# A skip sum moved from GpSimd to VectorE in the last layer of a graph network

## The reference

```python
x = _layernorm(x + attention(x, adj))          # stage 1
skip = x
for l in range(3):                             # stage 2, L = 3 layers
    si, sj = x @ attn_w[l, :d], x @ attn_w[l, d:]
    scores = leaky(si[:, :, None] + sj[:, None, :] + attn_b[l])
    attn = softmax(where(mask, scores, -inf))
    h = layernorm(x + attn @ x, g1[l], beta1[l])
    ff = gelu(h @ W1[l] + b1[l]) @ W2[l] + b2[l]
    x = layernorm(h + ff, g2[l], beta2[l])
out = _layernorm(skip + x)                     # the skip sum, its statistics, its normalization
```

## Time and profile before

| | before |
|---|---|
| median of 3 runs | 1709.91 us (1709.25 to 1709.99) |
| the profiled execution's own time | 1712.13 us |
| its span, first to last instruction | 1710.3 us |
| busy share of the span | PE 94%, DVE 77%, ACT 72%, POOL 78% |
| granted TensorE clock, mean | 0.98 |

### The profile page before, as it was taken

The page is one execution under the profiler, slowest core; times in us unless marked ns, Lnnn a source line. Parts: engine busy times, 40 slices in busy tenths (PEclk is TensorE's granted clock), DMA queues, the critical chain, the costliest instruction groups (busy, mean ns, idle before and its releaser), DMA issues.

```text
span 1710.3 us, 40177 instructions
## 1 busy us (share of the span) xinstructions
PE 1609.1 (94%) x11904; PEld 1425.8 (83%) x11904; DVE 1320.2 (77%) x5300; ACT 1230.9 (72%) x2855; POOL 1337.6 (78%) x2385
## 2 busy tenths in 40 slices
PE   4999999984999999999999999999999999999994
PEld 3888888872898998998898998988889888888894
DVE  1898898896777777777977777777888887888862
ACT  1888888883677677677777777776776777777763
POOL 5688888875478777787787787787778999999996
PEclk8999999996999999999999999999999999999997
DMA  6122332232022122122122221221220212222211
GB/s 200 64 93 93 98 98 90 87 106 80 26 99 91 44 74 74 37 74 73 38 75 72 88 74 38 72 74 37 74 73 26 86 65 95 74 74 79 69 50 49
DMA packets 145979, 127.50 MB, mean 75 GB/s; under 512 B 16512, under 2 KB 136832, under 8 KB 145920
## 3 DMA queue, kind: packets, MB, share of 16 engines
q1 hardware_dynamic: 138880, 124.30, 22.5%
q10 hardware_dynamic: 7040, 2.51, 0.6%
HBM read 89.04 MB, written 37.75 MB: 74 GB/s over the span
## 4 chain that ended last, share of the span: by engine, by line
PE 56%; POOL 13%; DVE 5%; issue 2%; ACT 1%; POOLq 0%; DVEq 0%; ACTq 0%
PE ps L45 24%; PE ps L894 24%; PE ps L866 4%; PE ps L880 2%; DVE gnn_junk L1026 2%; POOL xo L807 2%; POOL gnn_n L160 2%; POOL gnn_norm L801 2%; POOL gnn_fin L821 2%; POOL gnn_norm L160 2%; POOL inv L155 1%; PE ps L858 1%; POOL gnn_hb L790 1%; PE ps L873 1%; POOL gnn_hb L786 1%
## 5 line engine op out<-in xcount | busy, mean ns | idle before, releaser
L894 PE MATMUL ps<-gnn_w_hi,gnn_g_hi 128*128 128x256 f32 x1536 | 433.9, 282 | 0.0
L894 PE MATMUL ps<-gnn_w_lo,gnn_g_hi 128*128 128x256 f32 x1536 | 428.9, 279 | 0.0
L894 PE MATMUL ps<-gnn_w_hi,gnn_g_lo 128*128 128x256 f32 x1536 | 428.7, 279 | 0.0
L993 ACT ACTIVATE gnn_g_hi<-ps,b_cols 128x512 fp32r<-128x512 f32 x384 | 264.3, 688 | 200.1 <-PE ps L45 200.1
L1097 DVE TENSOR_TENSOR gnn_g_lo<-ps,gnn_g_hi 128x512 fp32r<-128x512 f32 x384 | 262.4, 683 | 101.6 <-ACT ps L994 101.0
L45 PE MATMUL ps<-gnn_hT_hi,gnn_w_hi 128*128 128x512 f32 x768 | 338.4, 441 | 0.0
L45 PE MATMUL ps<-gnn_hT_hi,gnn_w_lo 128*128 128x512 f32 x768 | 303.5, 395 | 0.0
L45 PE MATMUL ps<-gnn_hT_lo,gnn_w_hi 128*128 128x512 f32 x768 | 303.4, 395 | 0.0
L894 PEld LDWEIGHTS ps<-gnn_w_lo,gnn_g_hi 128*128 128x128 f32 x1536 | 288.9, 188 | 2.2
L894 PEld LDWEIGHTS ps<-gnn_w_hi,gnn_g_hi 128*128 128x128 f32 x1536 | 288.8, 188 | 2.2
L894 PEld LDWEIGHTS ps<-gnn_w_hi,gnn_g_lo 128*128 128x128 f32 x1536 | 288.7, 188 | 0.0
(11 more groups left out here) (127 smaller groups left out, 3979.4 us busy)
## 6 DMA issues: line engine op xcount, KB each, us to landing
hist<-xo SPq DMA_DIRECT2D x48, 512.0 KB, 3.9
x<-hist SPq DMA_DIRECT2D x48, 512.0 KB, 3.8
aw<-in_L_gnn_attn_w SPq DMA_DIRECT2D x48, 256.0 KB, 4.1
gmask<-mask_hist SPq DMA_DIRECT2D x48, 256.0 KB, 4.1
att_xT_raw<-in_xT SPq DMA_DIRECT2D x16, 512.0 KB, 3.3
att_xl<-in_x SPq DMA_DIRECT2D x16, 512.0 KB, 3.6
gnn_fin<-hist SPq DMA_DIRECT2D x16, 512.0 KB, 3.8
out<-gnn_fin SPq DMA_DIRECT2D x16, 512.0 KB, 3.0
```

What stands on the lines that cost most here:

```text
L894: mm = e.matmul(FF2[j % 2], g[a][:, m, j * N:(j + 1) * N], W2[b][:, m, :], start=(n == 0), stop=(n == len(terms) - 1))
L993: e.activation(g[0][:, m, :], FF1[FFB[m]], ACT.Gelu, bias=bias)
```

## The change

`final_sum` is taken out of POOL's step. `final_statistics(t-1)` on DVE, in step t, now waits for the load of `fin` and for `xo` of step t-1 (`x_out`), writes a one-column fence, makes the four sums itself, and then takes the statistics, each behind a wait for its sum. The wait for `fin_sum` is thus one within DVE.

```diff
-                def final_sum(t, par, half):
-                    e.wait_ge(fin_ld[par], 16 * (half - FIRST // 2 + 1))
-                    for j in range(GROUP):
-                        ins = e.tensor_tensor(fin[par][:, j, :], fin[par][:, j, :], xo[par][:, j, :], ALU.add)
-                    ins.then_inc(fin_sum, 1)
...
                     ln_ffn(2 * q + par, par, q, final >= 1)
-                    if final >= 1:
-                        final_sum(2 * q + par, par, q)
...
                 def final_statistics(q, par):
-                    t1, p1, _ = ahead(q, par, -1)
+                    t1, p1, h1 = ahead(q, par, -1)
                     n = t1 - FIRST
-                    e.wait_ge(fin_sum, n + 1)
-                    for j in range(GROUP):
+                    e.wait_ge(fin_ld[p1], 16 * (h1 - FIRST // 2 + 1))
+                    hold_dve(e, x_out, t1 + 1)
+                    for j in range(GROUP):
+                        e.tensor_tensor(fin[p1][:, j, :], fin[p1][:, j, :], xo[p1][:, j, :], ALU.add).then_inc(fin_sum, 1)
+                    for j in range(GROUP):
+                        e.wait_ge(fin_sum, GROUP * n + j + 1)
                         ins = e.bn_stats(st3[:, j, :], fin[p1][:, j, :])
                     ins.then_inc(bn3_out, 1)
```

## The result

The changed kernel takes 1738.44 us (1736.64 to 1739.19, 4 runs) where the kernel before took 1709.82 in the same comparison: a ratio of 1.0162, 95% interval 1.0150 to 1.0174, 28.6 us longer. The direction was forecast, the size was not: 14.5 us were predicted, and the time lies above the range, which ended at 1732.

A forecast was written before the change was run, and what follows sets the result against it. POOL was taken to bound eleven steps by a little, PE right behind. 25.4 us lost, 9.6 won, 1.3 won at the end: 14.5 us longer, 1724.4 us; range 1704 to 1732, the forecast's own 1719 to 1732.

The forecast's parts named there:

- What bounded the kernel, and what the change frees: Last layer: PE's transposes wait 9.6 us for POOL's n1; taking four sums a step off POOL frees that.
- The new wait: Steps 33 to 45: PE's transposes wait for DVE's probs_max, A - 1.0 us in each of 13 steps, 25.4 us lost.
- A: Time of DVE's four sums right behind residual2(t, 0), taken as 2.95 us, with 1.37 and 3.55 as ends.
- The clock: Last layer: PE's clock was assumed to stand a pause of 2 us; the forecast entered no cost for it.
- worse than the sum: Rival, 6%: PE's longer pauses or delays in DVE's step cost a further 0.5 us a step, 1731 us.
- The free run: Rival, 18%: DVE's sums run unhindered by POOL, A is 1.37, 6.1 us shorter, 1703.8 us.
- The balance: Rival, 14%: DVE's sums meet POOL's n1 instead of hb, A is some 1.8, no change, 1709.4 us.
- The alternation: Two-input work of DVE and POOL alternates and does not overlap; four such intervals make 3.55 us.
- The end: After the last xo, DVE's four sums and fence replace POOL's 2.77 us of sums: 1.3 us less.

## Why the prediction was wrong in size

**What bounded the kernel, and what the change frees.** Right. Without any sums 12.2 us are won; 9.6 and 2.8 had been read.

**The new wait.** Right: 13 steps, `probs_max`, and a delay of A - 1.0 each. At A = 3.34 and 3.41 the rule gives 2.3 to 2.4 us; the waits average 2.3. So the steps are some 28.3 us apart at the full clock, where 27.8 were forecast.

**The size of A.** Too small: 2.95 was taken, the mean of a burst wholly beside POOL's `hb` products (3.31) and of one that meets them halfway (2.59). Both kinds of step are like the first: 11 of the 13 bursts take 3.2 to 3.6 us, two take 2.99. I had put the start of `hb` at 0.4 and 0.7 us after `residual2(t, 0)`; it starts 1537.49 - 1537.39 = 0.10 and 1567.26 - 1567.10 = 0.16 us after it, and over the 13 steps between 0.3 us before it and 0.5 after. The gap between `n1` and `hb` is 0.08 us in the last layer's loop instead of the 0.22 of the second layer, which I carried over, and `mv2` ends 2.3 to 2.7 us after the start of the last matmul of PE's second product, instead of 2.9. By the burst of step 31 alone the sum would have had 13 x 2.31 = 30.0 us, which is what the waits came to. This term was short by 4.6 us; with it alone the sum would be 19.1 us longer, 1729, inside the range.

**The clock.** This is the step that failed: "PE's clock stayed at 1.00 through pauses of up to 1.4 us; I assume that it stands a pause of 2 us". It did not, in six steps of 13. That is 10.2 us of lower clock, which the sum had at nothing; with PE at work in the pauses the clock stayed at 1.00 and 8.7 us came back. The case stood among the rivals as "worse than the sum" at 6%, with "much more if the clock fell" and no number. The last layer's loop of the kernel before has no pause over 1.4 us, so its rows could not carry the assumption. Rows of another stage of the same trace spoke against it, and had the price. In stage 1, PE paused twice, for 0.47 and 1.03 us, between 380.3 and 383.4 us, and behind that the clock was at 0.50 for 3.41 us (windows of the kernel before):

```profile
380.30:383.72 3.42, 1.92 (x23) 1.32 (x16) 3.32 (x26) 2.16 (x12) 2.95 (x8) 1.00 0.00 0
383.72:387.13 3.41, 3.41 (x39) 2.49 (x38) 2.36 (x7) 3.14 (x16) 1.03 (x2) 0.50 0.42 139
```

The changed kernel has the same two pauses, and there the clock stayed at 1.00. So the length of a pause alone does not tell whether the clock falls, and "up to 1.4 us" was no safe bound either.

**The other rivals.** The free run (A = 1.37) exists: it is the run with one input in SBUF, 5.8 us less against 6.1 forecast. With both inputs in SBUF it needs POOL out of the way, which the changed kernel doesn't give. The balance did not come about; DVE's attention sums ran undisturbed and nothing pushed POOL later. With POOL held on purpose, A fell to 1.6 to 1.7, near the 1.8 of that case, and the time to 0.2% below before.

**The alternation.** "It does not overlap" was too strong. A sum of DVE starts every 0.88 us beside POOL's products; alone a sum takes 0.34 and a product 0.71, together 1.05. So part of an instruction does overlap; A came to 3.3 us where whole instructions in turn would have made it about 3.5.

**The end.** 1.3 us forecast, 1.4 found.

Together: 14.5 forecast, 4.6 from A, 10.2 from the clock: 29.3, against 28.6 measured.

## What to carry to other kernels

Moving work from the engine that is late to one that has time is worth at most the lateness, here 0.87 us a step, so move just so much: one sum of four took nearly all of it, and four lost three times as much. Before a two-input SBUF instruction goes to VectorE, look at what GpSimd does in that very stretch, and price it by a burst of the trace that has the same neighbour; if GpSimd has slack, a wait that keeps it out can be worth more than it costs. And where a change makes PE pause for longer than any pause in the trace, the price of the clock belongs into the sum with a number; another stage of the same trace may have it.

## What the runs showed of the hardware

- A sum of two 128 x 256 inputs on DVE took 415 ns with one of them in PSUM. With both in SBUF beside POOL's two-input work the sums started 0.88 us apart behind the first, and four in a row took 3.0 to 3.6 us; beside POOL's one-input `n1` four took 1.6 to 1.7, and beside an idle POOL 1.35. "SBUF — State Buffer" of the Trainium skill, section "Who interferes with whom", says that a DVE instruction with two SBUF inputs contends with a GpSimd instruction that reads SBUF, over ports that one of them holds exclusively. The runs agree on the contention. They differ in two things: an interval of 0.88 us is less than the 0.34 and 0.71 of the two instructions alone, and `n1`, which reads SBUF too, costs far less than work with two inputs.
- Of 13 pauses of PE of 1.7 to 2.3 us, one in each step of 28 to 30 us, six (2.1 to 2.2 us) were followed by a granted clock of 0.50 for 3.41 us, and seven were not. In the last layer the clock stayed at 1.00 through pauses of up to 1.4 us (kernel before, three sums on DVE); in stage 1 of the kernel before it fell behind pauses of 0.47 and 1.03. What decides it, and why it is every second step here, no run says.
